# Small root chains go from VectorE to GpSimd, and the second layer's modulation goes behind the third batch's exponentials

## The reference, cut to what matters

```python
mod = (_silu(L0_c) @ L0_wmod).reshape(16, 6, 1, -1)        # sa, ca, ga, sb, cb, gb; once for each layer
h = _layernorm(x) * (1 + ca) + sa
x = x + ga * attention_0(h)                                # 16 heads of 8 channels, causal
...
mod = (_silu(L1_c) @ L1_wmod).reshape(16, 6, 1, -1)        # the second layer's modulation
# inside attention_0
attn = softmax(causal(Q @ K.T * scale))
t = h @ dp_w1 + dp_b1                                      # 64 wide
t = (t - t.mean(-1)) / sqrt(t.var(-1) + 1e-5) * ln_g + ln_b   # the gate's own norm
gate = tanh(gelu((gelu(t) @ dp_w2 + dp_b2) * g_w1 + g_b1) @ g_w2 + g_b2)
out = (attn * gate) @ V @ Wo + bo
```

## Time and profile before

| what | value |
|---|---|
| time, median of 3 runs | 1044.93 us (1044.36 to 1049.99) |
| the profiled execution's own time | 1051.69 us |
| its span, first to last instruction | 1049.9 us |
| mean granted TensorE clock | 0.959 of full |
| busy: PE, PEld, DVE, ACT, POOL | 930.4, 756.7, 625.3, 569.4, 275.8 us |

### The profile page before, as it was taken

One profiled execution on the slowest core, in us unless ns is written; L12 is line 12 of the kernel. 1 busy time (PEld: TensorE's weight loads), 2 busy tenths in 40 slices (PEclk: granted clock), 3 DMA queues, 4 the chain that ended last, 5 costly groups with the idle time before them and its releaser, 6 DMA issues.

```text
span 1049.9 us, 20318 instructions
## 1 busy us (share of the span) xinstructions
PE 930.4 (89%) x7878; PEld 756.7 (72%) x7878; DVE 625.3 (60%) x1989; ACT 569.4 (54%) x965; POOL 275.8 (26%) x380
## 2 busy tenths in 40 slices
PE   4598899988989999999999999999999988968960
PEld 3354455545679888988888988888888876858860
DVE  8978787786559673654636545454654757812325
ACT  4478977776867655454545446455454546523320
POOL 4436431310201221203222112222112020364541
PEclk9699999999999999999999999999999998989995
DMA  5754441670940000000000000000000120212306
GB/s 142 203 142 123 120 115 46 186 218 20 292 110 1 2 1 1 1 1 22 1 21 1 7 16 2 21 1 18 4 2 21 41 77 24 55 54 67 105 28 219
DMA packets 81755, 66.41 MB, mean 63 GB/s; under 512 B 8666, under 2 KB 72184, under 8 KB 81660
## 3 DMA queue, kind: packets, MB, share of 16 engines
q1 hardware_dynamic: 76452, 56.44, 19.7%
q0 software_dynamic: 4320, 8.27, 2.4%
q10 hardware_dynamic: 888, 0.42, 0.1%
HBM read 33.78 MB, written 31.59 MB: 62 GB/s over the span
## 4 chain that ended last, share of the span: by engine, by line
PE 73%; ACT 9%; DVE 8%; issue 4%; SPq 4%; another core or an unknown queue 1%; DMA 1%; POOLq 0%; POOL 0%; DVEq 0%; ACTq 0%
PE psum L1449 26%; PE psum L1426 19%; PE psum L1269 3%; PE psum L1207 3%; DVE maxes L1797 2%; ACT big L2405 2%; PE psum L1501 2%; PE psum L1223 1%; PE psum L1250 1%; SPq L1063 1%; PE psum L1349 1%; PE psum L1199 1%; PE psum L1177 1%; ACT ew L2300 1%
## 5 line engine op out<-in xcount | busy, mean ns | idle before, releaser
L1449 PEld LDWEIGHTS psum<-ew,big 128*128 128x128 f32 x2560 | 321.1, 193 | 48.0 <-ACT big L2405 13.3
L1449 PE MATMUL psum<-ew,big 128*128 128x128 f32 x2560 | 330.7, 278 | 27.7 <-ACT big L2405 11.0
L2405 ACT ACTIVATE big<-psum,cols 128x512 f32<-128x512 f32 x256 | 174.5, 689 | 193.1 <-PE psum L1426 176.9
L1426 PE MATMUL psum<-parts,q_stack 128*128 128x512 f32 x640 | 221.0, 426 | 4.2 <-DVE parts L2146 2.4
L1952 DVE SCALAR_TENSOR_TENSOR hT<-psum,gates,hT 128x128 f32<-128x128 f32 x256 | 72.0, 344 | 98.5 <-PE psum L1449 84.5
L1797 DVE TENSOR_REDUCE maxes<-psum 128x4 f32<-128x1024 f32 (+1 forms) x96 | 114.2, 1218 | 21.5 <-PE psum L1223 21.3
L1426 PE MATMUL psum<-parts,k_stack 128*128 128x512 f32 x320 | 126.5, 395 | 0.0
L2691 POOL DMA_INDIRECT routed<-big,slot_i x64 | 62.7, 980 | 227.9 <-DVE slot_i L2141 156.4
L1426 PEld LDWEIGHTS psum<-parts,q_stack 128*128 128x128 f32 x640 | 105.4, 191 | 15.0 <-DVE parts L2146 2.6
L2701 POOL DMA_INDIRECT answers<-hT,to x64 | 62.5, 976 | 88.4 <-DVE hT L2160 67.8
L2412 ACT ACTIVATE big<-psum 128x512 f32<-128x512 f32 x64 | 38.1, 600 | 67.7 <-PE psum L1426 35.0
(11 more groups left out here) (403 smaller groups left out, 1564.6 us busy)
## 6 DMA issues: line engine op xcount, KB each, us to landing
q_stack<-q_pieces SPq DMA_DIRECT2D x32, 192.0 KB, 3.4
k_stack<-k_pieces SPq DMA_DIRECT2D x32, 192.0 KB, 4.6
routed<-empty_row SPq DMA_DIRECT2D x4, 1040.0 KB, 11.4
big<-routed SPq DMA_DIRECT2D x16, 260.0 KB
answers<-gb_tok SPq DMA_DIRECT2D x4, 1024.0 KB, 10.3
q_pieces<-gb_tok SPq DMA_DIRECT2D x16, 192.0 KB, 2.1
k_pieces<-gb_tok SPq DMA_DIRECT2D x15, 192.0 KB, 2.1
x<-in_L_attn_x SPq DMA_DIRECT2D x4, 512.0 KB, 6.0
```

The source lines that it names most:

```text
L1426: last = eng.matmul(bank(i), w1_part(wp, e)[:, fs], parts[2 * xk + xp][:, :], start=n == 0, stop=n == 2)
L1449: last = eng.matmul(psum[:, i, k * C:(k + 1) * C], hid[:, r, f, k * P:(k + 1) * P], ew2[:, e, f, :], start=f == 0, stop=f == FC - 1)
L2405: eng.activation(hid[:, held("hid", "up", n, e, f), f, :], bank(held("bank", "up", n, e, f)), ACT.Relu, bias=col("L0_ffn_b1", e * FC + f)) ...
```

## The change

1. The roots of groups 2, 3 and 4 of the first norm (batches 4 to 15) move to GpSimd as a new step `stat_p`. Its `rsqrt` has 11 instructions instead of 8, since the fused form of two operations is not used; with eps it is 12, and for group 2, which needs `shift`, 14. The plan costs it at 4 us on GpSimd, where `stat` was 2 us on VectorE.
2. `gv_s` keeps its sum on VectorE; the scale and the root (12 instructions) move to GpSimd. The plan costs it at 0.7 + 3.6 us instead of 3.
3. `wmod1` is planned behind TensorE's part of `exp` (2, 0) too. The function itself waits for nothing new.
4. `cut` of chunk 1 has urgency 10 instead of 3 in the plan.

```diff
+BY_POOL = (2, 3, 4)
+def first_stat(b):
+    g = first_group(b)
+    return ("stat_p", g) if g in BY_POOL else ("stat", 0, 0, g)
...
-    p.step("wmod1", work="sp:.6 dma:6", after=[(("mod", 0), "pe"), ("stack", 1, 1)])
+    p.step("wmod1", work="sp:.6 dma:6", after=[(("mod", 0), "pe"), ("stack", 1, 1), (("exp", 2, 0), "pe")])
...
-        p.step("stat", 0, 0, g, work="dve:2", urgent=4 if g == 1 else BACK, after=[("moment", b) for b in range(t0 // TPB, t1 // TPB)])
+        p.step(*first_stat(t0 // TPB), work="pool:4" if g in BY_POOL else "dve:2", urgent=4 if g == 1 else BACK,
+               after=[("moment", b) for b in range(t0 // TPB, t1 // TPB)])
...
-                p.step("cut", n, w, work="act:.53 pool:1.15", urgent=3, after=[("rest", n, w)], closes=[(1, tile)], tmp=tile)
+                p.step("cut", n, w, work="act:.53 pool:1.15", urgent=10 if n == 1 else 3, after=[("rest", n, w)], closes=[(1, tile)], tmp=tile)
...
-        p.step("gv_s", n, work="dve:3", urgent=0 if n else 8, after=[("gv_q", n)], tmp=tile)
+        p.step("gv_s", n, work="dve:.7 pool:3.6", urgent=0 if n else 8, after=[("gv_q", n)], tmp=tile)
...
@@ gv_s on VectorE
-                                  ALU.add).then_inc(chain.sem, chain.more())
-                w.wait_ge(chain.sem, chain.n)
-                eng.tensor_scalar(drift[:, ts], drift[:, ts], 1.0 / HID, EPS, ALU.mult, ALU.add).then_inc(chain.sem, chain.more())
-                w.wait_ge(chain.sem, chain.n)
-                rsqrt(drs[:, ts], drift[:, ts], dln_tmp[:, ts]).then_inc(sem("gv_s"), 1)
+                                  ALU.add).then_inc(sem("gv_s", "dve"), 1)
@@ on GpSimd
+            def rsqrt(y, v, t):
+                eng.tensor_scalar(y.bitcast(I32), v.bitcast(I32), -0.5, float(0x5F3759DF), ALU.mult, ALU.add).then_inc(chain.sem, chain.more())
+                w.wait_ge(chain.sem, chain.n)
+                eng.tensor_tensor(t, y, y, ALU.mult).then_inc(chain.sem, chain.more())
...
+                return eng.tensor_tensor(y, t, y, ALU.mult)
+            def stat_p(g):
+                ts = slice(*FIRST[g])
+                for b in range(FIRST[g][0] // TPB, FIRST[g][1] // TPB):
+                    w.wait_ge(*done("moment", b))
+                v = mv[:, ts, 1]
+                eng.tensor_scalar(v, v, EPS, None, ALU.add).then_inc(chain.sem, chain.more())
+                w.wait_ge(chain.sem, chain.n)
+                last = rsqrt(rstd[:, ts], v, ln_tmp[:, ts])
+                if FIRST[g][0] < BY_ACT * TPB:
...
+                    last = eng.tensor_scalar(shift[:, ts], shift[:, ts], -1.0, None, ALU.mult)
+                last.then_inc(sem("stat_p"), 1)
+            def gv_s(n):
+                ts = slice(n * GT, (n + 1) * GT)
+                w.wait_ge(*done("gv_s", n, by="dve"))
+                eng.tensor_scalar(drift[:, ts], drift[:, ts], 1.0 / HID, EPS, ALU.mult, ALU.add).then_inc(chain.sem, chain.more())
+                w.wait_ge(chain.sem, chain.n)
+                rsqrt(drs[:, ts], drift[:, ts], dln_tmp[:, ts]).then_inc(sem("gv_s"), 1)
```

More of the change, by code:

```diff
@@ L363, in normalise @@
         p.step(*normed(l, second, b), work=("act:.96" if b < BY_ACT else "pool:1.57") if first else "dve:.52", rank=rank, chain=chain,
-               after=[("stat", l, second, first_group(b) if first else b * TPB // LG), *after], opens=[(0, tile)], tmp=tile)
+               after=[first_stat(b) if first else ("stat", l, second, b * TPB // LG), *after], opens=[(0, tile)], tmp=tile)
         p.step("ln_t", l, second, b, work="pe:.6 act:.56" if first and b < 4 else "pe:.2 act:.47", after=[normed(l, second, b), ("mod", l)], rank=rank, chain=chain,
@@ L2244, in ln_a @@
                 k = held("tmp", "ln_a", b)
-                w.wait_ge(*done("stat", 0, 0, first_group(b)))
+                w.wait_ge(*done(*first_stat(b)))
                 for c in cleared("tmp", "ln_a", b):
@@ L2555, in late @@
                 eng.dma_start(wr[:, :], a["L1_ffn_w_router"]).then_inc(late_in, 16)
+            def rsqrt(y, v, t):
[3 more added lines that the diff above has]
+                w.wait_ge(chain.sem, chain.n)
+                eng.tensor_tensor(t, t, v, ALU.mult).then_inc(chain.sem, chain.more())
+                w.wait_ge(chain.sem, chain.n)
+                eng.tensor_scalar(t, t, -5.0 / 3.0, None, ALU.add).then_inc(chain.sem, chain.more())
+                w.wait_ge(chain.sem, chain.n)
+                eng.tensor_tensor(t, t, t, ALU.mult).then_inc(chain.sem, chain.more())
+                w.wait_ge(chain.sem, chain.n)
+                eng.tensor_scalar(t, t, 20.0 / 9.0, None, ALU.add).then_inc(chain.sem, chain.more())
+                w.wait_ge(chain.sem, chain.n)
+                eng.tensor_tensor(y, t, y, ALU.mult).then_inc(chain.sem, chain.more())
+                w.wait_ge(chain.sem, chain.n)
+                eng.tensor_tensor(t, y, y, ALU.mult).then_inc(chain.sem, chain.more())
+                w.wait_ge(chain.sem, chain.n)
+                eng.tensor_tensor(t, t, v, ALU.mult).then_inc(chain.sem, chain.more())
+                w.wait_ge(chain.sem, chain.n)
+                eng.tensor_scalar(t, t, -0.5 * 0.375 ** 3, 1.5 * 0.375, ALU.mult, ALU.add).then_inc(chain.sem, chain.more())
+                w.wait_ge(chain.sem, chain.n)
+                return eng.tensor_tensor(y, t, y, ALU.mult)
@@ new lines, in stat_p @@
+            def stat_p(g):
[4 more added lines that the diff above has]
+                eng.tensor_scalar(v, v, EPS, None, ALU.add).then_inc(chain.sem, chain.more())
+                w.wait_ge(chain.sem, chain.n)
+                last = rsqrt(rstd[:, ts], v, ln_tmp[:, ts])
+                if FIRST[g][0] < BY_ACT * TPB:
+                    last.then_inc(chain.sem, chain.more())
+                    w.wait_ge(chain.sem, chain.n)
+                    eng.tensor_tensor(shift[:, ts], mv[:, ts, 0], rstd[:, ts], ALU.mult).then_inc(chain.sem, chain.more())
+                    w.wait_ge(chain.sem, chain.n)
+                    last = eng.tensor_scalar(shift[:, ts], shift[:, ts], -1.0, None, ALU.mult)
+                last.then_inc(sem("stat_p"), 1)
@@ L2704, in send @@
                         oob_is_err=False).then_inc(answer_out[k], 16)
-            mine = {"masks": masks, "late": late, "ln_p": ln_p, "rest": rest, "cut": cut, "gv_a": gv_a, "gv_w": gv_w, "gv_v": gv_v, "ss_p": ss_p, "am_s": am_s, "blk": blk, "gam": gam_, "tab": tab,
+            mine = {"masks": masks, "late": late, "ln_p": ln_p, "stat_p": stat_p, "gv_s": gv_s, "rest": rest, "cut": cut, "gv_a": gv_a, "gv_w": gv_w, "gv_v": gv_v, "ss_p": ss_p, "am_s": am_s, "blk": blk, "gam": gam_, "tab": tab,
                     "la_g": la_g, "rt_d": rt_d, "send": send}
```

4 lines of the change are left out of this document (2 added, 2 removed).

## The result

The changed kernel takes 1051.93 us (21 runs, 1048.80 to 1056.96), the kernel before, beside it, 1048.38 (21 runs, 1043.19 to 1051.89): ratio **1.0043** (1.0029 to 1.0057). Forecast was 1042.5 in a range from 1034.5 to 1050.0, so the sign is wrong and the time is outside. Of the 9.4 us in between, 3.45 are the base (1044.93 was the median of three runs); the change itself was forecast at -2.4 us and is +3.55. The profiled executions differ less, 1052.11 against 1051.69 us (spans 1050.4 and 1049.9); the ratio is from the medians.

What follows compares the result with a forecast made beforehand. TensorE was taken as the bound almost everywhere, VectorE from 35 to 56 us. The terms -2.9 - 1.9 + 2.7 - 1.5 + 0.7 + 0.5 = -2.4 took the median 1044.93 to 1042.5 us, range 1034.5 to 1050.

Steps and rivals of the forecast that it cites:

- Part 1: Start: without group 2's and first gate's roots on VectorE, first maximum at 36.0 instead of 38.98; -2.9 us.
- The 0.8 for contention: 36 to 51 us: GpSimd's chains would hold up VectorE's three small two-input instructions; 0.8 us worse, left out of the sum.
- Part 2: 35 to 56 us: second layer's modulation leaves, first exponentials' products at 50.8 instead of 55.65; -1.9 us.
- Part 3: Behind the third batch: the modulation returns with the same 12 instructions where TensorE is 92% busy; +2.7 us.
- Part 4: 60 to 220 us: three gates' and groups 3 and 4's roots off VectorE shorten TensorE's waits; -1.5 us.
- Part 5: GpSimd's queue at the start: chunk 1's keys written about 6 us later, TensorE waits 0.7; +0.7 us.
- The cover for the first gate: In part 5: first gate ends near 53.4, first `pv` due at 55, so covered by 1.6 us.
- rival B: `cut` of chunk 1's keys waits behind 26 GpSimd links; at 0.6 a link +5.1 us, 1050.0; chance 0.15.
- Part 6: Last gate, near 223.4 us: its root ends 2.1 us later against 1.0 of slack; +0.5 us.
- rival A: 60 to 220 us: VectorE's relief carries through, modulation falls half into a gap; -8.5 us, 1036.4; chance 0.27.
- C: Start does not move, as key stack lands later or low clock lasts longer; +0.5 us, 1045.4; chance 0.13.
- 3 us either way: Allowance for the plan putting every later step in order anew, set with the 5.6 us spread of the runs.

Runs made afterwards that it cites:

- null_before: Kernel before with only the plan's cost of a first statistic on VectorE raised from 2 to 2.3, no instruction changed; ratio 1.0100 to the kernel before.
- stats_alone: Kernel before, all its lists kept, only the roots of groups 2 to 4 moved to GpSimd; ratio 0.9981 to the kernel before.
- gelu_first: Changed kernel, lists kept, first gate's gelu ahead of the first exponential and its last sum ahead of the second copy of maxima; ratio 1.0034 to before.
- fills_behind: Changed kernel, lists kept, two loads of expert weights put behind the last copy of maxima on SyncE's list; ratio 1.0035 to the kernel before.
- stats_fills: stats_alone with six of the eight exchange-buffer fills brought forward on SyncE's list; ratio 0.9949 to the kernel before, median 1008.29 us.
- stats_fills_again: The kernel stats_fills measured once more on another chip; ratio 0.9945 to the kernel before, median 1042.56 us.

## Why the prediction was wrong

- *Part 1, root chains off VectorE (-2.9).* Right to 0.3 us: the first maximum at 35.66, gated by the key stack, VectorE idle for 6.80 before it. Links of 0.28 us, 0.31 assumed. The 0.8 for contention, named there and left out of the sum, had no ground: GpSimd's chains end at 35.99, before the small VectorE instructions that it was worked out for.
- *Part 2, the modulation leaves (-1.9).* Right: the first exponential is 4.7 us sooner, -4.8 was forecast for parts 1 and 2 together.
- *Part 3, it comes back (+2.7).* Mis-sized: 12 products take 1.51 us at 86.58, at the full clock, where the earlier trace rows show 2.71 at the lower one.
- *Part 4, later roots off VectorE (-1.5).* No gain is seen. On old lists gates' chains on GpSimd put batch 3 at 106.9 instead of 106.3, although VectorE had less to do; with the stats' roots alone it was 102.6.
- *Part 5, GpSimd's queue (+0.7).* The order worked was exactly right. The cover for the first gate was not: it was priced at nothing to 3 us with 1.6 us of slack, and the gate came 8.5 us later than forecast. In the changed kernel that is the gelu's place on ScalarE. On old lists it is VectorE's wait of 2.79 us for the gate, a path that neither the part nor rival B had: B looked at the keys of chunk 1, for which TensorE never waited, and at the price of a link, which was 0.28. What cost was the second chain as a whole, not the price of its links.
- *Part 6, the last gate (+0.5).* Its case did not arise: the new lists end the last gate at 198.2 instead of 223.4.
- *Rivals.* A is not borne out: instead of 8.5 us in all, VectorE's relief was worth 0.2%, some 2 us, with the stats alone and the fills forward, and less than nothing with all roots moved. C is refuted at the start: the first maximum did move.

**The step that failed** is the sum itself: it carried each microsecond of the start through to the end, and allowed "3 us either way" for the plan's reordering, taken from the spread of the runs shown, which says nothing of reordering. The runs showed three things in its place. The first is the plan's order: null_before puts one such reordering at 1%, 10 us, and the new lists with the old roots cost 1.2%. The second is the floor: "TensorE is the bound almost everywhere" came from the busy share from 60 to 220 us and from the chain of waits around the start; between 259 and 302 us that chain lies on SyncE, and what is gained ahead of it is lost there (stats_alone, gelu_first, fills_behind). The third is the pair: the roots moved on unchanged lists give 1.0018, and either kind alone 0.9981 and 0.9974, where parts 1 and 4 had added both up as gains.

The mechanism forecast for the start was right, and the later loss is not a size but a path that the sum did not have. How the changed kernel's 3.55 us divide between order and floor stays open. Its last maxima came 2.4 us late in one trace and the addition 2.75, but the same kernel varied by 4.0 and 4.7 us between two traces. Why these lists end later though they were 15.5 us ahead at batch 5 is shown in part: fills_behind removes the stall of 5.44 us and ends the exponentials 9.9 us sooner. The rest is postponed values and projections, read from the traces and not tested. The range's lower half rested on rival A; that the result lies only 1.9 us above the range's end is no merit of rival B, whose mechanism did not occur.

## What to carry to other kernels

Read the chain of waits to the point where the gain should arrive, not only around the change; where the chain leaves the busiest engine for a queue of DMA issues, relief ahead of it may buy nothing (here 9.9 us at the last exponential did not). Where a planner orders the program, change one planned cost a little (2 to 2.3 us here) without changing an instruction, and take that difference as the size that a reordering can have, then pin the old lists to see what the edit is worth. Before two pieces of work are moved off a loaded engine, try each alone: one was enough here, and the second made the loaded engine wait for the other. And take a second trace of the same kernel before a difference of 2 us between two traces is called a cause.

## What the runs showed that I had not expected

- VectorE's small instructions of 0.17 us took 0.93 to 1.17 us beside GpSimd's 128x512 instructions with two inputs, and 0.16 to 0.19 beside GpSimd's chain of 128x8: a root costs 2.0 us or 6.5 by what GpSimd does meanwhile.
- GpSimd's links on 128x8 are 0.28 us from start to start, VectorE's 0.20: 1.4 times. The Trainium skill, "GPSIMD Engine Reference", section "4.1 Engine selection", speaks of about twice; for a chain this short the trace has less.
- The kernel before takes 1048 to 1050 us (medians) in four comparisons and 1014.16 in one, on another chip. The same kernel ran on both, as stats_fills and stats_fills_again: 1008.29 us on the fast chip and 1042.56 on one of the others, with the addition to x at 296.11 and 295.81, so the difference lies behind it. From 300 to 800 us TensorE is busy for 497.0 and 489.4 us; its expert products (L1479) wait 7.6 us for ScalarE there on the slower chip and not at all on the other. The rest of the 34 us arises after 800 us and is open. Ratios to a kernel run beside are therefore what is compared here.
